# Five GNN layers and a mixture of experts in one kernel: work moved between engines at the layer boundaries, an earlier check sum, and source one-hots in two wide instructions

## The reference

```python
# x [3125, 256]; 53125 edges src -> dst, sorted by dst; edge_attr [53125, 4]
h = layernorm(x)
norm = dinv[src] * dinv[dst]                        # dinv = deg ** -0.5
for l in range(5):
    edge_fea = concat([edge_attr[:, 3:] @ ew1[l], edge_attr[:, :3] @ ew2[l]], -1)
    agg = segment_sum(norm[:, None] * (h[src] + edge_fea), dst)
    h = relu(concat([h, agg], 1) @ mlp_w[l] + mlp_b[l])
    h = (h - h.mean(0)) * rsqrt(h.var(0) + 1e-5) * bn_g[l] + bn_b[l]
    if l != 4: h = relu(h)
x = x + h
x = x + moe(layernorm(x))                           # 8 experts, top 2
```

## Time and profile before

| | us |
|---|---|
| median of 3 runs | 1627.23 (1625.81 to 1627.88) |
| the profiled execution: its own time | 1623.4 |
| the profiled execution: its span | 1621.6 |
| PE busy in the span | 1414.7 (87%) |
| DVE busy in the span | 699.3 (43%) |
| ACT busy in the span | 403.4 (25%) |

### The profile page before, as it was taken

One profiled execution on the slowest core, in us unless ns is written; L12 is line 12 of the kernel. 1 busy time (PEld: TensorE's weight loads), 2 busy tenths in 40 slices (PEclk: granted clock), 3 DMA queues, 4 the chain that ended last, 5 costly groups with the idle time before them and its releaser, 6 DMA issues.

```text
span 1621.6 us, 25386 instructions
## 1 busy us (share of the span) xinstructions
PE 1414.7 (87%) x8976; PEld 849.7 (52%) x8977; DVE 699.3 (43%) x1919; ACT 403.4 (25%) x1045; POOL 173.5 (11%) x147
## 2 busy tenths in 40 slices
PE   2565589999889999989999899998999973899996
PEld 2554344444444544545445454454445452899995
DVE  6989999999722210122101220022200266343442
ACT  1320354343502400033001420014100241244342
POOL 1000000000000000000000000000000002477774
PEclk9876789999999999999999999999999966999998
DMA  5154000000000000000000000000000473144443
GB/s 129 51 162 154 1 2 1 1 2 1 15 1 0 14 0 1 1 13 1 0 1 1 13 0 1 0 1 14 1 0 22 85 251 118 39 69 71 68 74 43
DMA packets 49545, 57.77 MB, mean 36 GB/s; under 512 B 14319, under 2 KB 41601, under 8 KB 49184
## 3 DMA queue, kind: packets, MB, share of 16 engines
q1 hardware_dynamic: 38688, 41.67, 9.0%
q0 software_dynamic: 10752, 14.69, 5.6%
HBM read 42.36 MB, written 13.99 MB: 35 GB/s over the span
## 4 chain that ended last, share of the span: by engine, by line
PE 79%; DVE 13%; issue 3%; DVEq 2%; ACT 1%; DMA 1%; POOL 1%; SPq 0%; POOLq 0%
PE bank L674 33%; PE bank L767 13%; PE bank L683 9%; PE bank L1190 6%; PE bank L1199 6%; PE bank L1795 3%; DVE ohS L1557 2%; PE bank L664 2%; PE bank L1736 2%; DVE ohL L1443 1%; PE bank L689 1%; PE bank L1793 1%; PE bank L1181 1%; PE bank L1156 1%; DVEq L507 1%
## 5 line engine op out<-in xcount | busy, mean ns | idle before, releaser
L674 PE MATMUL bank<-at,m 125*128 125x500 fp8e4 (+1 forms) x2800 | 558.1, 355 | 0.0
L674 PEld LDWEIGHTS bank<-at,m 125*128 125x128 f16 x2800 | 254.8, 98 | 260.4 <-issue 14.9
L708 DVE TENSOR_TENSOR aggT<-bank,dinvB 128x500 f32<-128x500 f32 (+1 forms) x70 | 42.3, 622 | 379.3 <-PE bank L674 355.8
L862 ACT ACTIVATE hT<-bank,prm 128x500 f32<-128x500 f32 (+1 forms) x70 | 43.8, 633 | 573.6 <-PE bank L767 573.6
L683 PE MATMUL bank<-at,m 125*128 125x500 fp8e4 (+1 forms) x700 | 148.8, 364 | 8.0 <-issue 4.9
L911 POOL TENSOR_TENSOR idJ<-idJ,wts 125x1400 f32<-125x1400 f32 x2 | 8.0, 4008 | 1358.7 <-DVE idJ L1069 1358.7
L1557 DVE TENSOR_SCALAR ohS<-iotaS,now 128x128 bf16<-128x128 bf16 x504 | 117.8, 309 | 0.0
L767 PE MATMUL bank<-hT,wcur 128*128 128x500 f32 (+1 forms) x280 | 112.5, 545 | 2.2 <-DVE wcur L777 2.2
L1190 PEld LDWEIGHTS bank<-xtT,w1c 128*128 128x128 f32 x896 | 110.9, 195 | 2.8
L820 DVE BATCH_NORM_STATS2 zst<-hT 128x6 f32<-128x500 f32 (+1 forms) x70 | 43.5, 621 | 159.4 <-ACT hT L862 159.4
L635 DVE SCALAR_TENSOR_TENSOR m<-bank,dinvP,m 125x256 f16<-125x256 f32 x100 | 47.7, 483 | 148.2 <-ACT m L655 148.2
(11 more groups left out here) (310 smaller groups left out, 1373.1 us busy)
## 6 DMA issues: line engine op xcount, KB each, us to landing
slrow<-sl_dram SPq DMA_DIRECT2D x26, 512.0 KB, 5.1
w1s<-in_L_ffn_W SPq DMA_DIRECT2D x1, 4096.0 KB, 14.3
w2s<-in_L_ffn_W SPq DMA_DIRECT2D x1, 4096.0 KB, 19.8
xin<-in_x SPq DMA_DIRECT2D x1, 2800.0 KB
x<-in_x SPq DMA_DIRECT2D x1, 2800.0 KB
out_rows<-x SPq DMA_DIRECT2D x1, 2800.0 KB
xn_dram<-xn SPq DMA_DIRECT2D x1, 2800.0 KB
wraw<-in_L_gnn_mlp_w SPq DMA_DIRECT2D x5, 512.0 KB, 3.6
```

Of the source, the lines that this page charges most:

```text
L674: last = pe.matmul(bank[LATER[g % len(LATER)]][:, 0:w], m[:, s, k, h * 128:(h + 1) * 128], at_block(g // H)[:, s, :], start=False, stop=s ...
L862: act.activation(hT[:, h, a:a + w], bank[2 * (q % 2) + h][:, 0:w], ACT.Relu, bias=prm[:, 0, h:h + 1]).then_inc(s_z, 1)
```

## The change

**Between layers**, for the first two tiles DVE normalises the second half of the channels (a multiply-add, then a maximum, for each tile), ACT the first half alone and both tiles in a row; PE waits for both. For the last block of a layer DVE also takes the bias and ReLU of the second half. While PE would wait for the first tile it multiplies zeros, 14 matmuls of 500 columns.

**The check sum** over the counts is made before the last evictions, PE's part of it two groups ahead of the end, the flag before the last two evictions; `weights_dve` of the first layer comes ahead of the branch.

**Source one-hots** are made by two `tensor_tensor` of 1024 elements, a comparison ahead of the other one-hots and a product behind them, in pairs of chunks, so that the weights that PE reads are two elements apart.

```diff
+AIDED = 2
+ZC = H * NQ - 1
+WARM = 14
...
-        iotaS = r("iotaS", [128, 128], BF16)
+        iotaS = r("iotaS", [128, 128, 2], BF16)
...
-        ohS_1 = r("ohS_1", [128, U, 128], BF16)
+        ohS_1 = r("ohS_1", [128, U // 2, 128, 2], BF16)
...
         def m_rows_dve(dve, base):
+            for t in range(AIDED):
+                half = hT[:, 1, t * P:(t + 1) * P]
+                dve.tensor_scalar(half, half, cf[:, 4, 1:2], cf[:, 5, 1:2], ALU.mult, ALU.add).then_inc(s_hm, 1)
+            for t in range(AIDED):
+                half = hT[:, 1, t * P:(t + 1) * P]
+                dve.wait_ge(s_hm, base(AIDED) - AIDED + t + 1)
+                dve.tensor_scalar(half, half, 0.0, None, ALU.max).then_inc(s_hd, 1)
...
-                if t < 3:
-                    normalise(t)
+                if t == 0:
+                    normalise(0)
+                    normalise(1)
                 if t == 2:
+                    normalise(2)
                     normalise(3)
...
+            if t < AIDED:
+                pe.wait_ge(s_hd, prev(AIDED) + t + 1)
...
             for g in range(4):
                 attributes(pe, g, LATER, True)
+            pe.wait_ge(s_z, prev(ZC) + H * (NQ - 1))
+            for n in range(WARM):
+                pe.matmul(bank[3][:, 0:CQ], zeros[:, 0:128], nought(CQ), start=True, stop=True)
...
+                if q == NQ - 1:
+                    dve.wait_ge(s_mlp, base(H * NQ) + H * NQ)
+                    step(dve.tensor_scalar(hT[:, 1, a:a + w], bank[2 * (q % 2) + 1][:, 0:w], prm[:, 0, 1:2], 0.0, ALU.add, ALU.max))
+                    step(dve.bn_stats(zst[:, 1, q, :], hT[:, 1, a:a + w]))
+                    dve.wait_ge(s_z, base(ZC) + ZC)
+                    step(dve.bn_stats(zst[:, 0, q, :], hT[:, 0, a:a + w]))
...
-                for h in range(H):
+                for h in range(1 if q < AIDED and not last_layer else H):
                     last = act.activation(hT[:, h, a:a + w], hT[:, h, a:a + w], ACT.Identity if last_layer else ACT.Relu,
...
-                    dve.wait_ge(s_now[side], past + i + 1)
+                    dve.wait_ge(s_now[side], (past + i) * 2 + 1)
+                    dve.tensor_tensor(ohS[side][:, :, :, :], to_all(iotaS[:, :, :], U // 2), by_pairs(now[:, side, 12, :], 128), ALU.is_equal).then_inc(s_now[side], 1)
...
-                    for j in range(U):
-                        last = dve.tensor_scalar(ohS[side][:, j, :], iotaS[:, :], now[:, side, 12, j:j + 1], now[:, side, 13, j:j + 1], ALU.is_equal, ALU.mult)
-                    last.then_inc(s_oh[side], 1)
+                    dve.wait_ge(s_now[side], (past + i) * 2 + 2)
+                    dve.tensor_tensor(ohS[side][:, :, :, :], ohS[side][:, :, :, :], by_pairs(now[:, side, 13, :], 128), ALU.mult).then_inc(s_oh[side], 1)
...
-            for g in range(evicted, H * NQ):
-                evict(dve, zero, g, FIRST)
             dve.wait_ge(s_at, PAIRS)
             dve.tensor_reduce(bad[:, :], sums[:, :], axis=XYZ, op=ALU.add).then_inc(s_flagp, 1)
+            for g in range(evicted, H * NQ - H):
+                evict(dve, zero, g, FIRST)
+            weights_dve(dve, LOADS)
             dve.wait_ge(s_flagp, 2)
             dve.tensor_scalar(flag[:, :], bank[0][0:1, 0:1], float(E), None, ALU.not_equal).then_inc(s_flag, 1)
+            for g in range(H * NQ - H, H * NQ):
+                evict(dve, zero, g, FIRST)
...
-                        last = pe.matmul(out_w, ohS[side][:, j, :], cnt1[side][:, j // 2, :, j % 2].rearrange("p (g n) -> p g n", g=GROUPS),
+                        last = pe.matmul(out_w, ohS[side][:, j // 2, :, j % 2], cnt1[side][:, j // 2, :, j % 2].rearrange("p (g n) -> p g n", g=GROUPS),
...
-            dense_to(DENSE)
             pe.wait_ge(s_flagp, 1)
             pe.matmul(bank[0][0:1, 0:1], ones[0:P, 0:1], bad[:, :], start=True, stop=True).then_inc(s_flagp, 1)
+            dense_to(DENSE)
```

More of the change, by code:

```diff
@@ L191, in gnn_ffn_program @@
         r = Region((NT * 6 * CQ + 31) // 32 * 32)
-        ohS_0 = r("ohS_0", [128, U, 128], BF16)
+        ohS_0 = r("ohS_0", [128, U // 2, 128, 2], BF16)
         ohD_0 = r("ohD_0", [128, U // 2, W, 2], BF16)
@@ L401, in gnn_ffn_program @@
         s_h = sem("s_h")
+        s_hm = sem("s_hm")
+        s_hd = sem("s_hd")
         s_ls = sem("s_ls")
@@ L762, in linear_pe @@
                 if q >= 2:
-                    pe.wait_ge(s_z, base(H * NQ) + H * (q - 1))
+                    pe.wait_ge(s_z, base(ZC) + H * (q - 1))
                 for k in range(2 * H):
@@ L817, in statistics_dve @@
             for q, (a, w) in enumerate(COLS):
-                for h in range(H):
-                    dve.wait_ge(s_z, base(H * NQ) + H * q + h + 1)
-                    last = dve.bn_stats(zst[:, h, q, :], hT[:, h, a:a + w])
-                    if q == NQ - 1:
-                        step(last)
-                        dve.sem_inc(s_apart, 1)
-                        last = dve.bn_aggr(zmv[:, h, :], zst[:, h, :, :].rearrange("p q s -> p (q s)"))
+                if q == NQ - 1:
[4 more added lines that the diff above has]
+                    step(dve.bn_stats(zst[:, 0, q, :], hT[:, 0, a:a + w]))
+                else:
+                    for h in range(H):
+                        dve.wait_ge(s_z, base(ZC) + H * q + h + 1)
+                        dve.bn_stats(zst[:, h, q, :], hT[:, h, a:a + w])
+            dve.sem_inc(s_apart, 1)
+            for h in (1, 0):
+                last = dve.bn_aggr(zmv[:, h, :], zst[:, h, :, :].rearrange("p q s -> p (q s)"))
             last.then_inc(s_bv, 1)
@@ L859, in linear_act @@
             for q, (a, w) in enumerate(COLS):
-                for h in range(H):
+                for h in range(H if q < NQ - 1 else 1):
                     act.wait_ge(s_mlp, base(H * NQ) + H * q + h + 1)
@@ L866, in linear_act @@
             act.activation(cf[:, 1, :], zmv[:, :, 1], ACT.Sqrt, bias=eps[:, :]).then_inc(s_bs, 1)
-        LAYER_STEPS = 22
+        LAYER_STEPS = 23
         FW = 16 * (3 + 1 + NE)
@@ L1297, in _ @@
             pool.iota(iotaK[:, :, :], pattern=[[KEY, GROUPS], [1, W], [0, 2]], base=0, channel_multiplier=0)
-            pool.iota(iotaS[:, :], pattern=[[1, 128]], base=0, channel_multiplier=0, allow_small_or_imprecise_dtypes=True).then_inc(s_mem, 1)
+            pool.iota(iotaS[:, :, :], pattern=[[1, 128], [0, 2]], base=0, channel_multiplier=0, allow_small_or_imprecise_dtypes=True).then_inc(s_mem, 1)
             pool.memset(zt[:, :], 0.0).then_inc(s_cst, 1)
@@ L1588, in _ @@
                         aggregate_dve(dve, layer(l), LOADS * (l + 1))
-                    else:
-                        weights_dve(dve, LOADS)
                     statistics_dve(dve, layer(l), layer(l + 1) if l + 1 < L else None)
```

## The result

The change makes the kernel faster: a median of 1605.08 us (1601.15 to 1611.95, 4 runs) against 1627.56 (1625.81 to 1627.90) for the kernel before on the same chip, a ratio of 0.9868 [0.9837, 0.9898]. A second comparison gave 1606.47 against 1626.96, 0.9872 [0.9856, 0.9887]. The forecast was 1602, the range 1592 to 1614. The profiled execution of the first comparison is its slowest run (1611.95, a span of 1610.3).

What follows compares the result with a forecast made beforehand. PE was taken as the bound (79% of the chain, DVE 13%), losing time idle or at 1.2 GHz. Terms 13.1 + 3.6 + 3.2 + 5.2 = 25.1 us, from 1627.2 to 1602, range 1592 to 1614.

Steps and rivals of the forecast that it cites:

- Boundaries, 13.1: Four boundaries between layers: earlier first column and full PE clock held by zeros save 2 x 2.9 + 2 x 3.7 us.
- Tile 0 starts 0.25 earlier: At each layer boundary, splitting normalisation between ACT and DVE lets PE start its first tile 0.25 us sooner.
- Check sum, 3.6: End of the building: linear part starts 2.7 us sooner, 1.5 of clock returns, less 0.3 each for two delays.
- Early turns, 3.2: Windows 0 to 15, bound by DVE: seven turns with nibbles give 2.7 us, shorter way to last one-hots 0.55.
- The model of the sequencer: DVE's early turns: limit loads and loop entry after the product's wait set turns of about 3.5 us, 3.9 with nibbles.
- Four stalls, 5.2: Later building: PE's four waits for one-hots shrink, 2.2 us in all, plus part of the 6 us of clock loss.
- I take half of that as saved: Behind the four one-hot waits: half of about 6 us lost to half clock comes back once waits are 1.2 us.
- Rival 1: DVE's sequencer is not in the way: early turns give 9.3 us, shorter waits keep the clock; 1593 us, chance 0.17.
- Rival 2: At boundaries zeros do not hold the clock, or transposes lose it: 5 us there in all; 1610 us, chance 0.13.
- Rival 3: Strided source weights load slower on PE in windows 16 to 62, adding 36 us: 1638 us, chance 0.05.
- Rival 4: DVE's new one-hot instructions run bf16 at one element at a time, turns grow 0.6 us: about 1620, chance 0.03.
- The rule on transposes: Skill's rule that transposes do not count as clock work: some 2 us from last zeros to first column would be idle.

Runs made afterwards that it cites:

- experiment 3: Kernel before with only the two wide one-hot instructions: 1620.99 us, ratio 0.9961 to the kernel before.
- experiment 8: Kernel before with only the check-sum part: 1622.29 us, ratio 0.9977 to the kernel before.
- experiment 10: Kernel before with only the part between layers (zeros, DVE's halves, DVE's share of the last block): 1614.57 us, ratio 0.9940 to the kernel before.
- experiment 2: Kernel after without the 14 matmuls on zeros (WARM = 0): 1615.98 us, ratio 0.9925 to the kernel before.
- Experiment 7: Kernel after with ACT alone normalising both halves of the first two tiles, zeros and all else kept: 1612.08 us, ratio 0.9917 to the kernel before.
- experiment 4: Kernel after with the loads of the next window's limits moved ahead of the product's wait: 1599.42 us, ratio 0.9825 to the kernel before.
- Experiment 12: Kernel after with five matmuls of zeros ahead of turns whose one-hots PE waits for: 1605.51 us, ratio 0.9874 to the kernel before.
- experiment 5: Kernel after with five units of aggregation in each window in place of six (DENSE_W 5): 1591.95 us, ratio 0.9788 to the kernel before.
- experiment 6: Kernel after with both the limit loads moved ahead of the product's wait and DENSE_W 5: 1585.15 us, ratio 0.9751 to the kernel before.
- experiment 9: Kernel before with DENSE_W 5 in place of 6 and nothing else: 1614.65 us, ratio 0.9938 to the kernel before.

## Why the prediction was right, and which terms were off

The direction, the order of the three parts and the time (3 us off, inside the range) were right, and each part gave time by itself (experiments 3, 8 and 10). The sum was too high: 25.1 were forecast, 20.5 to 22.5 came by the medians. By the cuts of the second comparison it is 11.5 + 2.4 + 1.9 + 1.7 = 17.5 against the one profiled execution of before. That one had lain below its median, and I had moved the sum up to the median unchanged. The executions of before differ in the stretches at half clock (the layers took 814.2 to 816.5 us in the four profiles whose boundaries are as before), those with the zeros do not (802.3 in every one whose other two parts are in as well). The change thus takes more from a median execution than from a good one. That is argued; which stretches a median execution of before has was not profiled. That the forecast came within 3 us is thus partly luck: against the one profiled execution of before the four terms are 7.6 too high, and the larger gain of the medians makes up for 3 to 5 of that.

- **Boundaries, 13.1: measured 11.5.** That tile 0 to tile 4 falls to 7.0 was right (7.05), and that zeros hold the clock too (experiment 2). Wrong was "Tile 0 starts 0.25 earlier". From the end of the last linear matmul it is 522.17 to 526.80 = 4.63 now, and was 527.06 - 522.54 = 4.52: it starts 0.1 later. DVE's two multiply-adds stand ahead of its first maximum, so its halves end no earlier than ACT's two did, and the share of the last block costs 0.1 instead of nothing. Experiment 7 shows both: without DVE's halves, but with its share of the last block, it is 4.62. Four times 0.35 is 1.4 of the missing 1.6. The last linear matmuls of PE, kernel after, then kernel before:

```profile
521.11 1.06 PE L786 MATMUL bank<-aggT,wcur 128*128 128x125 f32 x8
```

```profile
521.48 1.06 PE L767 MATMUL bank<-aggT,wcur 128*128 128x125 f32 x8
```

- **Check sum, 3.6: measured 3.7** by the ratio (experiment 8), and 2.4 between the profiled executions of before and after. The clock's part, 1.5, is 803.8 - 802.3 between experiment 10 and the kernel after. In the kernel after PE loses 1.4 of it at the eviction's wait, where the fifty matmuls take 12.1. That happens with the one-hots alone too (12.24 in experiment 3), and not in experiment 7 (10.74), which has the order of the kernel after there, nor with the check sum alone: the reduction ahead of the eviction does not decide it. What does is open.
- **Early turns, 3.2: measured 1.9.** The model of the sequencer was right to 0.05 us for turns of 3.43 and 3.95, and experiment 4 shows it by moving the loads. Off was the count: seven turns with nibbles were taken, at 3.95. Ahead of the first unit stand five, and two of them take 4.4, since their `encB` starts 0.4 late; why is open.
- **Four stalls, 5.2: measured 1.7.** The step that failed is "I take half of that as saved". The waits became 0.6 shorter, as said; of the clock next to nothing came back (over the four stretches of 20 us 0.91 each before; 0.83 each in the first execution, three times 0.91 and once 1.00 in the second). Experiment 12 shows that it would have brought little more against the second: DVE's next turn is the bound behind it.
- **Not in the sum.** The wait of 5.20 for the attribute sums and the slow fifty matmuls behind it were in no term. The change did not touch them, so the forecast did not suffer.
- **The rivals.** Rival 1 fell, as the turn is set by the sequencer; but its price was right for what is to be had there (5.6 for 6.1). Rival 2 fell (experiment 2); its mechanism shows at two of the four boundaries of experiment 7, where gaps of up to 1.32 follow the zeros. Its price was a little low: without zeros the boundaries give 13.0 - 9.1 - 1.5 = 2.4, not 5. Rival 3 fell: eight source matmuls take 1.08 with strided and 1.07 with adjacent weights at full clock, and a load of weights takes 98 ns (median, the row of the kernel after below) where it was 96. Rival 4 fell: 0.69 for 1024 elements.

```profile
L1819 PEld LDWEIGHTS bank<-cnt,ohS x504: 96/98/149, 170.8 to 438.1; 128*128 128x128 bf16 x168
```

- **The rule on transposes.** Transposes alone ran between the last zeros and the first column, and PEclk stayed 1.00 there (524.00 to 531.00 above). The Trainium skill (TensorE: Matmul & The Clock Gate, Part 4, on transposes) would have that stretch count as idle; by that a loss was possible, and the trace shows none. In experiment 7 it is longer, 2.7 us at the fourth boundary (1092.83 to 1095.54), and there the clock fell at two of four boundaries. But its idle time is longer too, so no run separates the transposes from the idle time, and the rule itself is not tested.

## What to carry to other kernels

Before making an engine's instructions shorter, see what its sequencer does between them: loads that stand behind the last wait of a loop can set its length, and here moving three of them gave as much (7.1 us by the medians of one chip) as rewriting the instructions (6.3). Where PE shares windows with another engine, give each window the same amount of PE's work: windows without any cost more here (13.7 us for one digit, by the ratios) than the wide one-hots saved (6.3). Filling PE's idle time with zeros pays where PE itself is the bound behind the gap (9.1 us between layers), and paid little where another engine set the pace (experiment 12).

## What was not expected of the hardware

- With zeros and DVE's halves, the steps from one layer's first linear matmul to the next are 190.0 at every boundary (190.05 at most), in all executions with all three parts; without zeros they lay between 191.7 and 193.2 in one.
- The clock's answer to a gap is not the same each time. In experiment 7 waits of 0.59 and 1.32 were followed by half clock at two boundaries and by full clock at two. The wait for the eviction (1.94 to 2.17) was followed by full clock in the kernel before and in experiments 5 to 10, and by half clock in the kernel after (both profiles) and in experiments 2 to 4 and 12.
- Weights with elements two apart in bf16 cost PE next to nothing: eight matmuls 1.08 in place of 1.07.
